# A graph attention layer on one core: the second slot table has 19 chunks per block in place of 20

## The reference

```python
h = relu(layernorm(x))
q, k, v, hn = h @ Wq + bq, h @ Wk + bk, h @ Wv + bv, h @ Wn + bn
attn_in = concat([q[src], k[dst], edge_attr @ We + be])
hmid    = leaky_relu(attn_in @ A1 + b1, 0.2)
scores  = leaky_relu(hmid @ A2 + b2, 0.2)          # 8 heads
w       = softmax(scores.mean(-1), over all edges)
out     = segment_sum(w[:, None] * v[dst], src)
y       = hn + out
result  = x + gamma * (y - mean(y)) / sqrt(var(y) + 1e-5) + beta
```

## Time and profile before

| | |
|---|---|
| Median of 3 runs | 6895.85 us |
| Profiled execution, its own time | 6902.11 us |
| Its span, first to last instruction | 6900.3 us |
| Mean granted TensorE clock | 0.864 of full speed |
| Busy share of the span | PE 75%, PEld 59%, DVE 59%, ACT 42%, POOL 46% |
| Moved | 1288.94 MB, mean 187 GB/s |
| A unit's loads in the tail | u_rows 258.0 KB, q_bits 96.0 KB |
| TensorE busy by 40 slices, in tenths | 7454457777777777777777777777777777699787 |
| VectorE, likewise | 7444445555555565555555555555555555477999 |

### The profile page before, as it was taken

One profiled execution on the slowest core, in us unless ns is written; L12 is line 12 of the kernel. 1 busy time (PEld: TensorE's weight loads), 2 busy tenths in 40 slices (PEclk: granted clock), 3 DMA queues, 4 the chain that ended last, 5 costly groups with the idle time before them and its releaser, 6 DMA issues. The chain is left out here.

```text
span 6900.3 us, 138364 instructions
## 1 busy us (share of the span) xinstructions
PE 5145.5 (75%) x35486; PEld 4047.6 (59%) x35875; DVE 4067.4 (59%) x9754; ACT 2910.1 (42%) x7064; POOL 3200.1 (46%) x3381
## 2 busy tenths in 40 slices
PE   7454457777777777777777777777777777699787
PEld 4343345555566666666566666666666665477776
DVE  7444445555555565555555555555555555477999
ACT  4232223333444444444444444444444443334666
POOL 3665565555544455545554554554554555400000
PEclk9777778888888888888888888888988888899999
DMA  7566656666777766666566656666666665488888
GB/s 228 159 192 191 197 184 188 195 190 197 211 205 204 206 183 171 172 172 176 169 178 175 172 164 175 175 174 173 181 178 173 178 172 152 136 221 229 221 236 221
DMA packets 1963709, 1288.94 MB, mean 187 GB/s; under 512 B 637802, under 2 KB 1856017, under 8 KB 1963532
## 3 DMA queue, kind: packets, MB, share of 16 engines
q1 hardware_dynamic: 1793189, 844.54, 48.1%
q0 software_dynamic: 154752, 435.99, 17.2%
q10 hardware_dynamic: 15592, 6.41, 0.4%
HBM read 716.22 MB, written 570.23 MB: 186 GB/s over the span
## 5 line engine op out<-in xcount | busy, mean ns | idle before, releaser
L1243 POOL DMA_INDIRECT slots<-rows,slot_i x3224 | 3108.4, 964 | 2755.3 <-ACT rows L1388 1518.2
L1299 PE MATMUL ps_row<-win,mixed 128*128 128x256 f32 x5904 | 1599.9, 417 | 128.3 <-ACT rows L1388 54.6
L1388 ACT ACTIVATE rows<-ps_row 128x512 f32<-128x512 f32 x1476 | 892.8, 605 | 1345.6 <-PE ps_row L1299 669.1
L834 DVE TENSOR_SCALAR onehot<-ps_ls,part 128x512 bf16<-128x512 bf16 x670 | 322.8, 482 | 1915.2 <-ACT heads L796 816.8
L1299 PEld LDWEIGHTS ps_row<-win,mixed 128*128 128x128 f32 x5904 | 1173.2, 211 | 327.8 <-issue 94.3
L823 ACT ACTIVATE low<-ps_z 128x512 f32<-128x512 f32 x882 | 528.5, 599 | 1886.2 <-remote 1068.2
L1333 PE MATMUL ps_rank<-early_v,early_spot 128*128 128x128 f32 x3920 | 736.9, 353 | 335.6 <-issue 191.1
L1333 PEld LDWEIGHTS ps_rank<-early_v,early_spot 128*128 128x128 f32 x3920 | 671.8, 259 | 412.0 <-issue 250.5
L1270 PE MATMUL ps_e<-ident,edges 128*128 128x128 f32 x3224 | 591.0, 305 | 428.2 <-issue 144.0
L1270 PEld LDWEIGHTS ps_e<-ident,edges 128*128 128x128 f32 x3224 | 453.4, 158 | 667.1 <-issue 367.0
L753 PE MATMUL ps_z<-onehot,q_bits 128*128 128x512 bf16 x2257 | 694.4, 404 | 151.8 <-issue 137.6
(11 more groups left out here) (217 smaller groups left out, 5643.5 us busy)
## 6 DMA issues: line engine op xcount, KB each, us to landing
u_rows<-slots SPq DMA_DIRECT2D x1026, 258.0 KB, 3.2
early_v<-slots SPq DMA_DIRECT2D x490, 258.0 KB
edges<-edge_attr_dram SPq DMA_DIRECT2D x403, 256.0 KB
q_bits<-qb_tab SPq DMA_DIRECT2D x882, 96.0 KB, 3.2
v_own<-slots SPq DMA_DIRECT2D x248, 258.0 KB, 3.5
slots<-no_row SPq DMA_DIRECT2D x98, 528.0 KB
slots<-rows,slot_i POOLq DMA_INDIRECT x3224
slots<-no_row SPq DMA_DIRECT2D x98, 396.0 KB
```

The lines of the kernel that those rows point to most:

```text
L1243: pool.indirect_dma_start(slots_tab[h], bass.IndirectOffsetOnAxis(slot_i[:, u, j:j + 1], 0), rows[:, u, j, :], None).then_inc(scattered[u] ...
L1299: last = pe.matmul(bank[:, j % 2, :], mixed[:, u % 2, j, :], win[:, u, :], start=True, stop=True)
L1388: nc.scalar.activation(rows[:, u, 2 * k:2 * k + 2, 0:2 * U0].rearrange("p j (a c) -> p j a c", a=2)[:, :, :, 0:D], row_bank(s, k).rearrang ...
```

## The change

`CAPS[1]` goes from 20 to 19 chunks, `FILLED[1]` from 16 to 15, and the border `CUT` from group 178 to 184, a multiple of four, so that the scatter's loops need no group written out at it. The number of passes stays 9. In the last pass (8) a unit has `SHORT` = 3 chunks: `chunks` and `rows_at` give the count, and every operation over a unit's chunks takes it. In the score tail units 114 to 211 are short; as this must be known when a body is written, `score_steps` now has a loop over bodies 1 to 8, body 9 by itself, and a loop over bodies 10 to 15. In the weighted sum every fourth unit is short: VectorE makes two of its one-hots, ScalarE the third.

```diff
-CAPS = (16 * P, 20 * P)
-FILLED = (13, 16)
+CAPS = (16 * P, 19 * P)
+FILLED = (13, 15)
 TAILS = (3, 4)
-CUT = 178
+CUT = 184
-PASSES = FIRST_PASSES + CAPS[1] // (UNIT * P)
+PASSES = FIRST_PASSES + -(-CAPS[1] // (UNIT * P))
+SHORT = CAPS[1] // P - (PASSES - 1 - FIRST_PASSES) * UNIT
...
+        SHORT_FROM = NT * (PASSES - 1) - INSIDE
+        short_units = [False]
+        def chunks_of(p):
+            return SHORT if p == PASSES - 1 else UNIT
+        def chunks(o, i, k):
+            if o.inside:
+                return UNIT
+            short = i * o.units + k >= SHORT_FROM if known(i) else short_units[0]
+            return SHORT if short else UNIT
+        def last_with(o, i, k, c):
+            m, n = k % BATCH, batch_size(o, i, k)
+            return all(chunks(o, i, k - m + e) <= c for e in range(m + 1, n))
... load_unit
-            sp.dma_start(o.u_rows[:, r, :, :],
-                         slots_tab[h][bass.ds(row, UNIT * P), :]...
+            n = chunks_of(p)
+            sp.dma_start(o.u_rows[:, r, 0:n, :],
+                         slots_tab[h][bass.ds(row, n * P), :]...
... spread_lo, make_z, heads
-            for c in range(UNIT):
+            for c in range(chunks(o, i, k)):
... make_z, with w = chunks(o, i, k); scale_z, one_of and leaky_z likewise
-                last = pe.matmul(o.ps_z[:, k % n, :, :]..., o.onehot[:, k % one, :, :]...
+                last = pe.matmul(o.ps_z[:, k % n, 0:w, :]..., o.onehot[:, k % one, 0:w, :]...
... heads
-                                 start=(m == 0), stop=(m == batch_size(o, i, k) - 1), skip_group_check=True)
+                                 start=(m == 0), stop=last_with(o, i, k, c), skip_group_check=True)
... scatter loops on GpSimd
-                        looped(pool, EARLY, CUT - 2, lambda s, u: scatter(s, u, 0))
+                        looped(pool, EARLY, CUT, lambda s, u: scatter(s, u, 0))
                         pool.wait_ge(emptied[1], 16 * NT)
-                        one_by_one(CUT - 2, CUT + 2, lambda s, u: scatter(s, u, 0 if s < CUT else 1))
-                        looped(pool, CUT + 2, LOOPS_END, lambda s, u: scatter(s, u, 1))
+                        looped(pool, CUT, LOOPS_END, lambda s, u: scatter(s, u, 1))
... score_steps
+            border = SHORT_FROM // o.units
             for k in range(o.units):
                 step(0, k)
-            with eng.Fori(1, LEFT - 2) as i:
+            short_units[0] = False
+            with eng.Fori(1, border) as i:
+                for k in range(o.units):
+                    step(i, k)
+            for k in range(o.units):
+                step(border, k)
+            short_units[0] = True
+            with eng.Fori(border + 1, LEFT - 2) as i:
                 for k in range(o.units):
                     step(i, k)
...
+        def rows_at(k):
+            return SHORT if k % LATE == LATE - 1 else UNIT
... load_values
+                    n = rows_at(k)
-                    sp.dma_start(v_rows(r),
-                                 slots_tab[h][bass.ds(first, UNIT * P), :]...
+                    sp.dma_start(v_rows(r)[:, 0:n, :],
+                                 slots_tab[h][bass.ds(first, n * P), :]...
... sum_step on TensorE
-                    for c in range(UNIT):
+                    for c in range(rows_at(k)):
... place_last on ScalarE
-                    g, c = i * PAIR + k, UNIT - 1
+                    g, c = i * PAIR + k, rows_at(k) - 1
... place on VectorE
-                    for c in range(UNIT - 1):
+                    for c in range(rows_at(k) - 1):
```

More of the change, by code:

```diff
@@ L743, in make_z @@
             g, n = i * o.units + k, o.ps_z.shape[1]
-            r, one = o.u_rows.shape[1], o.onehot.shape[1]
+            r, one, w = o.u_rows.shape[1], o.onehot.shape[1], chunks(o, i, k)
             pe.wait_ge(o.u_in[k % r], in_count(o, i, k))
@@ L747, in make_z @@
                 pe.wait_ge(o.mid_ready, g - (n - 1))
-            for c in range(UNIT):
+            for c in range(w):
                 pe.matmul(o.ps_z[:, k % n, c, :], o.u_rows[:, k % r, c, 1:U0], ident[:], is_transpose=True,
@@ L752, in make_z @@
             for m in range(BITS):
-                last = pe.matmul(o.ps_z[:, k % n, :, :].rearrange("p c e -> p (c e)"), o.q_bits[:, k % r, m * D:(m + 1) * D],
-                                 o.onehot[:, k % one, :, :].rearrange("p c e -> p (c e)"), start=False,
+                last = pe.matmul(o.ps_z[:, k % n, 0:w, :].rearrange("p c e -> p (c e)"), o.q_bits[:, k % r, m * D:(m + 1) * D],
+                                 o.onehot[:, k % one, 0:w, :].rearrange("p c e -> p (c e)"), start=False,
                                  stop=(m == BITS - 1), skip_group_check=True)
@@ L822, in scale_z @@
                 act.wait_ge(o.mid_ready, g - (n - 1))
-            nc.scalar.activation(o.low[:, k % n, :, :], o.ps_z[:, k % o.ps_z.shape[1], :, :], ACT.Copy, scale=SLOPE
+            w = chunks(o, i, k)
+            nc.scalar.activation(o.low[:, k % n, 0:w, :], o.ps_z[:, k % o.ps_z.shape[1], 0:w, :], ACT.Copy, scale=SLOPE
                                  ).then_inc(o.low_ready, 1)
@@ L1778, in score_steps @@
         def score_steps(eng, step):
+            border = SHORT_FROM // o.units
+            assert 1 < border < LEFT - 3 and 3 <= SHORT_FROM - border * o.units <= o.units - BATCH
             for k in range(o.units):
                 step(0, k)
-            with eng.Fori(1, LEFT - 2) as i:
+            short_units[0] = False
[6 more added lines that the diff above has]
+            with eng.Fori(border + 1, LEFT - 2) as i:
                 for k in range(o.units):
@@ L2243, in sum_step @@
                         pe.wait_ge(y_chain, i * (6 * BLOCKS) + (6 * (k // LATE) - 10))
-                    for c in range(UNIT):
+                    for c in range(rows_at(k)):
                         last = pe.matmul(ps_y[:, b, 0:D], spot[:, k % SPOTS, c, :], v_rows(k % VRING)[:, c, 0:D],
-                                         start=(k % LATE == 0 and c == 0), stop=(k % LATE == LATE - 1 and c == UNIT - 1),
+                                         start=(k % LATE == 0 and c == 0), stop=(k % LATE == LATE - 1 and c == SHORT - 1),
                                          skip_group_check=True)
```

10 lines of the change are left out of this document (6 added, 4 removed).

## The result

| | before | after |
|---|---|---|
| Median, 6 runs each | 6914.95 us | 6864.67 us |
| Range | 6891.75 to 6929.34 | 6853.43 to 6888.36 |
| Profiled execution: own time, span | 6902.11, 6900.3 | 6871.36, 6869.5 |

The medians are 50.3 us apart. The ratio of the runs is 0.9919, 95% interval 0.9899 to 0.9939, which is 42 to 70 us. Predicted were 49.6 us less and 6846.3 us; the time lies inside the stated range. It is 18.4 us above the forecast, because the median of before has itself risen by 19.1 us: its six runs are the three of 6891.75 to 6908.71 us shown earlier and three more of 6921.19 to 6929.34.

What follows compares the result with a forecast made beforehand. TensorE was taken to bound the score tail and VectorE the weighted sum. Terms of 32.3 + 18.7 - 0.4 - 1 = 49.6 us, against the median of 6895.85, gave 6846.3 us, range 6824 to 6880.

Steps and rivals of the forecast that it cites:

- Tail, TensorE: Score tail: a short unit saves TensorE 0.33 us in transposes, matmuls and spreads, 32.3 us over 98 units.
- Heads: Score tail: the head matmuls of a short unit, six records instead of eight, save 0 us.
- rival A: Score tail: head records cost time one by one, so 6.2 us more gain, 6840 us; chance 0.10.
- Border of the tail's loops: Score tail, loop cut in two: one more loop entry costs 0.4 us, bounds 0 to 1.
- Weighted sum: Last stage: VectorE's dropped one-hots, limited by its waits on ScalarE, save 0.78 us per four blocks, 18.7 us in all.
- The ring through y_std: Weighted sum: VectorE's o_sb, ScalarE's store and y_std, VectorE's y_rstd wait in a circle; 19.73 us per four blocks.
- Between the stages: Tail to weighted sum: first blocks' values queue behind the tail's last loads, 1 us lost, bounds 0 and 2.
- Mixed stage: Before the tail: moving the border from group 178 to 184 costs 0 us, bounds -3 to +6.
- D: Mixed stage: the second table's 19-chunk spacing slows its transfers; 6878 us at 0.9%, 6923 at 2.3%; chance 0.13.
- B: Weighted sum: ScalarE is the wall, gain 12 us in place of 18.7, 6853 us; chance 0.13.
- C: Weighted sum: VectorE alone sets the pace, gain 25 us, 6840 us; chance 0.08.
- E: Tables: they overflow and the slow branch runs, over 12,000 us; chance 0.01.

Runs made afterwards that it cites:

- e11: The changed kernel, unedited, run again beside the kernel before: 6861.61 us, ratio to before 0.9932.
- e10: The changed kernel with its two tail loops kept but all units of four chunks: 6867.81 us, one run.
- e9: The changed kernel with the tail's q_bits loads for the unit six ahead issued by ScalarE instead of SyncE: 6856.36 us, ratio to before 0.9930.
- e12: The changed kernel with the edits of e4 and e9 together: 6848.67 us, ratio to before 0.9909.
- e4: The changed kernel with ScalarE's square root y_std one pair of one-hot instructions earlier: 6848.90 us, ratio to before 0.9918.
- e3: The kernel before with only the border moved to group 184 and the changed kernel's scatter loops: 6896.26 us, ratio to before 0.9995.
- e5: The changed kernel with the second table's blocks 20 chunks apart in memory as before: 5494.67 us on a faster chip, ratio to before 0.9919.
- e2: The changed kernel with the score tail computing all four chunks in one loop again: 6881.76 us, ratio to before 0.9970.
- e7: The kernel of e4 with GpSimd's xb addition cut to one column, beta left out of the output: 5484.57 us, one run on a faster chip.

## Why the prediction was right

**The total: right in its parts, and in part lucky.** 49.6 us were forecast, 50.3 lie between the medians. But the two stages are only 44.6 us shorter by their profiles and 41.7 in e11, and the medians of e11 and its kernel before are 44.1 apart. Both stages gave some 2.5 us less than predicted; what fills the gap is the scatter of the mixed stage and of the runs.

**Tail, TensorE: right.** 0.33 us per short unit as worked out from the earlier trace rows, batches of 5.33 against 5.31.

**Heads: right, and rival A is out.** Three groups of 32 columns cost what four cost: 1.00 against 1.01 us per batch. The match with 0.130 us per full-width record in the earlier trace rows was the right reason. By the Trainium skill ("TensorE: Matmul & The Clock Gate", "Part 3: Packing small matmuls — row/col tiling") one group less is worth some 4 ns; the trace agrees within what it resolves, 0.01 us over four units.

**Border of the tail's loops: the place was right, the path wrong and the size too small.** I had charged 0.4 us for one more entry into a loop. By itself that is free beside full units (e10), but it brings slow issues on SyncE, and there they meet a queue that needs 1.27 us for a unit used up in 1.33. The loss in the changed kernel is 2.5 us at the border, and 0.3 us near the end (2.6 in e11). e9, with half of the issues taken from SyncE, loses 0.2 us at the border and nothing near the end; but it also puts q_bits on another queue, and e12, with the same edit, still loses 1.0 and 1.9 us behind loads that landed late. So SyncE's pace is shown for the border of the changed kernel, by its chain; near the end the late loads are what the chains show, and their cause is open. I had checked VectorE, ScalarE and the DMA share against the new pace of 1.33 us, and not SyncE's instructions, though I had DMA issues in view for ScalarE. This is the term that was mis-sized: 31.9 predicted for the tail, 29.5 measured.

**Weighted sum: right mechanism.** The ring through y_std was predicted at 19.73 us per body and stands at 19.81 in the first loop; e4, which takes it out, gives 19.46 against the 19.48 for VectorE alone. VectorE's one-hots number 1078 in place of 1176, the 98 fewer that were forecast. What I missed is that the second loop is not the first one: it was at 20.81 before and I had read only the first. There 0.54 us per body were won and not 0.78: two blocks of four gained 0.24 and 0.26, the one with the jump nothing, since the ring binds it, and the one before it 0.04, since its acc_sb now takes 0.60 us in place of 0.35 (below). With 12 bodies of 0.70 and 10 of 0.54 the loops give 13.8 us, and 15.1 were measured for the stage; 18.7 - 1 were predicted.

**Between the stages: 1 us predicted.** The first o_sb of the weighted sum starts 24.0 us after the last maximum, 23.5 before: 0.5 us.

**Mixed stage: nothing, as predicted.** e3 for the border (0.9995), e5 for the stride. I had written that D was right if the stage's end moved by more than 10 us. It moved by 13.8, and D was not right: over ten profiles that end scatters by 37 us, so the sign was drawn too tight. Rivals B, C, D and E are out: B by e4 and the store at 0.23 us, C by e4, D by e5, E by the run itself.

## What to carry to other kernels

When a stage gets faster, redo the sum for every queue that must keep up, and take a queue that only issues DMAs by its pitch from issue to issue: here 1.27 us stood ready behind a pace of 1.33, and no busy share showed it. Look too at how long the loads take to land around the places where the engines enter new code (up to 6 us here, 3 elsewhere), since a ring of buffers must bridge that. When two engines hand something back and forth once per block, add up the ring from one trace; here it gave the new body of four blocks as 19.73 us where 19.81 were measured, and it also named the edit (the square root one place earlier) that took the ring away. Read each loop of a stage by itself. And before a moved time is made a sign, find out how far it moves between runs of one kernel.

## What the runs showed of the hardware

**VectorE beside GpSimd.** In the second loop of the changed kernel two instances of VectorE's acc_sb (L2589):

```profile
6741.41 0.35 DVE L2589 SCALAR_TENSOR_TENSOR acc_sb<-acc_sb,part_inv,part_in  x1
...
6746.32 0.60 DVE L2589 SCALAR_TENSOR_TENSOR acc_sb<-acc_sb,part_inv,part_in  x1
```

and GpSimd's xb (L2179) beside them:

```profile
6741.51 0.57 POOL L2179 TENSOR_TENSOR xb<-x_rows,beta_b 127x128 f32<-127x128 f32 x1 [4.37 <-DVE o_sb L2617]
6746.32 0.45 POOL L2179 TENSOR_TENSOR xb<-x_rows,beta_b 127x128 f32<-127x128 f32 x1 [4.25 <-DVE o_sb L2617]
```

Where GpSimd's operation starts 0.10 us after acc_sb, acc_sb takes 0.35 us. Where both start at 6746.32, acc_sb takes 0.60. GpSimd's own takes 0.57 and 0.45. In the whole trace nine acc_sb take some 0.6 us, all at one place of the second loop's body, and they are the nine that start within 0.03 us of an xb; before and in e2 none start so close and none takes over 0.5. In e7, with xb cut to one column, nine start as close and take 0.35. Which of the two happens depends on a tenth of a microsecond, so the same code can settle into bodies of 20.27 (changed kernel) or 20.06 us (e2), and cutting GpSimd's operation down brought 19.60 (e7).

**The mixed stage on another chip.** 3500 us of the kernel before:

```profile
1000.00:4500.00 3500.00, 2673.03 (x18071) 2104.11 (x18303) 1962.34 (x4209) 1461.17 (x3579) 1806.94 (x1878) 0.86 0.64 184
```

and of e5_stride20 in the second call:

```profile
1000.00:4500.00 3500.00, 3050.49 (x24022) 2540.21 (x24325) 2583.63 (x5565) 1973.70 (x4873) 2351.05 (x2444) 0.96 0.80 235
```

The granted clock is 0.96 in place of 0.86, and in the same time 1.33 times the matmuls are done (24022 against 18071), at 235 in place of 184 GB/s. The clock is only 1.12 times as high, so it doesn't account for the 1.33 by itself; the runs don't show what else does. These are two kernels, but the same holds for one: the kernel before has a mean granted clock of 0.94 over its whole execution on that chip and 0.86 on the others. The kernel before took 5540.40 us on that chip in place of some 6905, while in e5 tail and weighted sum were as long (330.7 and 508.3 us) as in the changed kernel on the other chips (331.6 and 510.5). Why the chip grants more there was not tried. The gain in microseconds was the same in both places: 46 there (e5, the changed kernel with the old stride) and 44 to 50.
